# Gated cross attention and routed FFN on one core: small jobs put between the two halves of a step, numerators laid over denominators by DMA

## The chip, the cores and the metric

The kernel runs on one core of a Trainium2 chip, in one launch. The metric is the device time of the launch in microseconds (us). The core's engines are PE (TensorE, matrix products and transposes), ACT (ScalarE), DVE (VectorE), POOL (GpSimd) and SP (SyncE, which here only issues DMA transfers). Each engine carries out its own list of instructions in order; semaphores make one engine wait for another or for a DMA. Three times were taken of the kernel before: 714.03, 714.83 and 716.48 us, median 714.83.

## The reference, cut to what matters

`x` and `ctx` are 16 x 128 x 512 (batch, channel, position), float32.

```python
h = _layernorm(x)                     # over the 512 positions
qh = h.reshape(16, 8, 16, 512)        # 8 heads of 16 channels
kh = vh = ctx.reshape(16, 8, 16, 512)
sm = softmax(einsum('bhdq,bhdl->bhql', qh, kh) * scale, axis=-1)
ret = einsum('bhql,bhdl->bhdq', sm, vh).reshape(16, 128, 512)
x = x + tanh(g_xattn[0]) * gamma * ret
x = x + tanh(g_ffn[0]) * ffn(_layernorm(x))
```

`ffn` is a routed feed-forward block of eight experts, two per token, with a shared branch; the change doesn't touch it.

## The kernel before

**Stages.** The attention over 16 batches comes first and takes some 400 us; then the FFN for four groups of tokens. The change is in the attention.

**Windows.** Attention goes in windows w = 0 to 17 (with a short lead-in, w = -1). All engines run the same windows: `over_windows` lays out w = -1 to 3 one after the other, then a loop of five turns of two windows each (w = 4 to 13, the pair of bodies is that of w = 4 and 5), then w = 14 to 17. In window w a batch is at several stages at once: the maxima of batch w, the exponentials of batch w-1 (from step 7 of the window before on) and, one step behind them, its products with the values, the division and residual of batch w-2, the second layernorm of batch w-3, and keys and queries of batch w+1.

**A step on PE.** `pe_jobs` writes a window as eight steps s of two halves. A half step is: two matmuls of transposed scores (`st`), each into one of three PSUM slots called the ring; one pair of matmuls of scores in natural order (`nat`), of which DVE takes one row maximum `mx` (16 a window, k = 0 to 15, eight for each group g of heads); and four matmuls of exponentials with values (`pv`). In the step of the last keys of a group all eight `pv` come at the end of the step. Two other jobs use ring slots too: `m` transposes the 8 maxima of a group into a row, and `vt` transposes 128 x 512 context in two halves into values. ACT frees a ring slot: `st` by an exponential into `P`, `m` by writing `mrow` (times -1), which ACT then lays into row 48 of the query stack `QS` by DMA, `vt` by two copies into `VT` a half. PE waits for a slot that was used three jobs before (`ring_free`). The row of g = 0 is needed by the `st` of step 7 (ahead of k = 14), that of g = 1 by those of step 3 of the next window (k = 6). The order on ACT follows `pe_jobs`.

**Sums.** `VT` holds 16 columns of values and 16 of ones alternately, so that the sums `pv` hold in 32 partitions of a head pair 16 numerators and 16 equal denominators. For one group of heads the numerators are below, for the other above. ACT copies the sums of the two groups to `U0` and `U1`. SP stores the denominators (`den_scratch`), loads them back packed (`dc`), DVE takes the reciprocal after a fixed maximum (`PLACED`), SP stores it and loads it broadcast (`rd`). POOL masks both sums with `cme` (the gate in one half of the rows, 0 in the other) and adds them (`na`, `nb`, `num`), multiplies with `rd` (`att`), and adds `x` (`x1`).

**Order of the rest.** DVE puts its small jobs behind maxima by the table `PLACED`, POOL's list is `pool_jobs`, SP's is the body in `sync`. `Fori` loops run the two bodies with registers as indices. `tail` holds pieces of the second stage that are placed in the windows, on SP the zeroing of `y_sums` ("zeros"), four transfers a window from w = 3.

Of the kernel before, what the change touches and what calls it, by code (L numbers as in the profile page):

```python
# [28 lines left out]
P = 128  # L29
# [202 lines left out]
def attention(nc, c, keep, sb, ps, sem, x, ctx_kv, gx, gf, gamma, wall, const, ones, x1s, us, sq, sk, sd):  # L232
# [29 lines left out]
    cme = A("cme", [P, 2])  # L262
# [16 lines left out]
    t_st, t_xr, t_us = T("x1_out", 16), T("x_again", 16), T("u_out", 16)  # L279
    t_nat, t_ring, t_pv = T("pe_nat"), T("pe_ring"), T("pe_pv")  # L280
# [11 lines left out]
    def pe_jobs(w):  # L292
        jobs = []
        for s in range(STEPS):
# [11 lines left out]
            if s == 0 and 1 <= w <= B:  # L306
                jobs.append(("m", w - 1, 1))
            if s == 1 and w < B:
                jobs += [("vt", w, 0), ("vt", w, 1)]
            if s == 4 and w < B:  # L310
                jobs.append(("m", w, 0))
# [25 lines left out]
    def pool_jobs(w):  # L337
        jobs = []
        if 2 <= w < B + 2:
            jobs += [(w - 2, n) for n in ("na", "nb", "num")]  # L340
        if w + 1 < B:
            keys, queries = ("kh", "kl"), ("negm", "veps", "rstd", "rs", "qf", "qh", "ql")
            jobs += [(w + 1, n) for n in (("rstd",) if w < 0 else keys + queries)]
        if w >= 3:
            jobs += [(w - 3, n) for n in ("xnegm", "xveps", "xrstd", "u", "x1t")]
        if 0 <= w < B:
            jobs += [(w, "whi"), (w, "wlo")]
# [4 lines left out]
    for w in range(-1, B + 3):  # L352
# [15 lines left out]
        if 2 <= w < B + 2:  # L368
            t_ds.plan(w - 2, n=2)
            t_rb.plan(w - 2)  # L370
# [25 lines left out]
    def sync(sp, tail):  # L396
# [33 lines left out]
        def body(ck, w):  # L430
# [13 lines left out]
            if t >= 0:  # L444
                ck.wait(t_ev, t, 1)
                for g in range(2):
                    r = DH * (1 - g)
                    sp.dma_start(sd[ck.index(t), 0].rearrange("(j g) q -> g j q", g=2)[g], U[g][r:P:32, :]).then_inc(t_ds.sem, 16)
# [7 lines left out]
            if t >= 0:  # L456
                ck.wait(t_pool, t - 1, "x1")
                sp.dma_start(xr[:, :], x[ck.index(t)]).then_inc(t_xr.sem, 16)
# [28 lines left out]
            if 0 <= w and b < B:  # L487
                stack(ck, b, 0, 0)
            if s >= 0:
# [5 lines left out]
            if b < B:  # L495
                stack(ck, b, 1, 1)
                stack(ck, b, 1, 0)
# [96 lines left out]
    def scalar(act, tail):  # L594
# [20 lines left out]
        def value_sums(ck, b, s):  # L615
            ck.wait(t_pv, b, s)
            ck.wait(t_pool, b - 1, "nb")
            ck.wait(t_ds, b - 1)
            act.copy(U[s // 4][:, :], pv[:, :]).then_inc(t_ev.sem, 1)

        def body(ck, w):
# [3 lines left out]
            for kind, b, *rest in pe_jobs(w):  # L625
# [30 lines left out]
                else:  # L656
                    a, = rest
                    src = bank[:, 0:2 * P].rearrange("p (l j g d) -> p l g j d", l=2, g=2, d=DH)
                    for g in range(2):
                        m = act.copy(VT[i][:, 2 * a:2 * a + 2, g, :, DH * g:DH * g + DH], src[:, :, g, :, :])  # L660
# [9 lines left out]
    def vector(dve, tail):  # L670

        PLACED = {1: ("stats",), 2: ("aggr",), 5: ("recip",), 6: ("xstats",), 7: ("xaggr",)}
# [57 lines left out]
    def gpsimd(pool, tail):  # L730
        pool.memset(minus_half[:, :], -0.5).then_inc(t_vt.sem, 1)
        def job(ck, b, what):
# [3 lines left out]
            if what == "na":  # L736
                ck.wait(t_ev, b, 1)
                ck.wait(t_pool, b - 1, "att")
                done(pool.tensor_scalar(tn[:, :], U[0][:, :], cme[:, 0:1], 1.0, ALU.mult, ALU.mult))
            elif what == "nb":  # L740
                ck.wait(t_st, b - 2)
                done(pool.tensor_scalar(ao[i][:, :], U[1][:, :], cme[:, 1:2], 1.0, ALU.mult, ALU.mult))
            elif what == "num":
                ck.wait(t_pool, b, "nb")
                done(pool.tensor_tensor(tn[:, :], tn[:, :], ao[i][:, :], ALU.add))
            elif what == "att":
                ck.wait(t_rb, b)
                ck.wait(t_pool, b, "num")
                done(pool.tensor_tensor(ao[i][:, :], tn[:, :], rd[:, :], ALU.mult))  # L749
# [62 lines left out]
        def body(ck, w):  # L812
# [4 lines left out]
            if w < 0:  # L817
# [7 lines left out]
                pool.wait_ge(t_gate.sem, 2)  # L825

                pool.tensor_scalar(cme[:, 0:2], cst[:, K_ME:K_ME + 2], gate[:, 5:6], None, ALU.mult).then_inc(t_gate.sem, 1)
                pool.wait_ge(t_gate.sem, 3)
# [1436 lines left out]
```

## Time and profile before

| | us |
|---|---|
| median of three runs | 714.83 |
| lowest, highest | 714.03, 716.48 |
| profiled execution, its own time | 716.26 |
| its span in the trace | 714.4 |
| PE busy | 662.5 (93%) |
| ACT busy | 531.0 (74%) |
| DVE busy | 512.4 (72%) |
| POOL busy | 464.7 (65%) |

Busy times are for the whole span. In the attention windows all four engines are busy most of the time; in the second stage PE is, and the others less.

### The profile page before, as it was taken

What the parts mean: (1) busy time and instruction counts of PE and PEld (TensorE: products, weight loads), DVE (VectorE), ACT (ScalarE), POOL (GpSimd) and SP (SyncE); (2) the same over time, 40 slices, a digit from 0 to 9 for tenths busy, and PEclk for the clock granted to TensorE, in tenths of its full rate; (3) what the DMA queues carried; (4) which work ended last, traced back from release to release, by engine and by line L of the source; (5) the groups of instructions that cost most, each with busy time, mean ns of one, the idle gap of its engine ahead of it and who ended that gap; (6) DMA issues with size and microseconds to landing.
All of it is one profiled execution on the core that took longest, in us unless ns stands there. A gap on an engine that the chain in (4) does not pass through costs nothing. (4 is left out here: it accounts for less than half of the span.)

```text
span 714.4 us, 20683 instructions
## 1 busy us (share of the span) xinstructions
PE 662.5 (93%) x6005; PEld 352.7 (49%) x6005; DVE 512.4 (72%) x859; ACT 531.0 (74%) x1125; POOL 464.7 (65%) x464
## 2 busy tenths in 40 slices
PE   1798998899999999999999998879999999999998
PEld 0122222233333233322345554448999999998744
DVE  4988999899999999999878665564444444444456
ACT  2398998799999999999888467448777777677411
POOL 3557698888889888886846713404566665675622
PEclk9999999999999999999999999989999999999999
DMA  6646575656666566565334652448989779677587
GB/s 201 212 139 192 181 237 155 216 179 205 207 222 193 180 214 204 183 193 169 125 117 160 218 182 104 164 110 148 189 111 137 122 121 131 94 115 98 58 274 269
DMA packets 128176, 120.15 MB, mean 168 GB/s; under 512 B 64100, under 2 KB 97636, under 8 KB 128104
## 3 DMA queue, kind: packets, MB, share of 16 engines
q1 hardware_dynamic: 114680, 104.09, 50.1%
q0 software_dynamic: 12192, 14.16, 12.8%
q10 hardware_dynamic: 1232, 0.98, 0.4%
q8 instruction: 40, 0.66, 0.4%
q14 instruction: 32, 0.26, 0.1%
HBM read 60.25 MB, written 49.10 MB: 153 GB/s over the span
## 5 line engine op out<-in xcount | busy, mean ns | idle before, releaser
L716 DVE TENSOR_REDUCE mx<-nat 128x2 f32<-128x1024 f32 x256 | 296.6, 1213 | 24.3 <-PE nat L545 23.2
L641 ACT ACTIVATE P<-ring 128x512 f32<-128x512 f32 x512 | 279.4, 603 | 20.4 <-PE ring L557 10.4
L2229 POOL DMA_INDIRECT y_sums<-ysb,to x74 | 124.4, 1681 | 91.9 <-DVE ysb L2163 74.1
L570 PE MATMUL pv<-P,VT 128*32 128x256 f32 x2048 | 159.1, 395 | 0.4
L545 PE MATMUL nat<-KS,QS 48*128 48x512 f16 x512 | 111.9, 398 | 25.8 <-DMA QS<-q_scratch 15.0
L557 PE MATMUL ring<-QS,KS 49*128 49x512 f16 x512 | 123.5, 393 | 8.6 <-ACT P L641 8.6
L1331 PE MATMUL EH<-XA,whi 128*128 128x256 f16 (+1 forms) x688 | 104.5, 258 | 0.0
L1331 PE MATMUL Y<-whi,u 128*128 x592 | 104.0, 273 | 0.1
L570 PEld LDWEIGHTS pv<-P,VT 128*32 128x32 f32 x2048 | 44.1, 109 | 92.5 <-issue 44.6
L2113 DVE TENSOR_TENSOR u<-X,u 128x512 f16<-128x512 f32 x62 | 42.7, 689 | 64.6 <-ACT u L1737 64.6
L557 PEld LDWEIGHTS ring<-QS,KS 49*128 49x128 f16 x512 | 32.2, 93 | 111.7 <-ACT P L641 94.7
L1331 PE MATMUL EH<-XA,wlo 128*128 128x256 f16 (+1 forms) x344 | 84.5, 258 | 0.0
L1331 PE MATMUL Y<-wlo,u 128*128 x296 | 80.7, 273 | 0.0
L1731 ACT ACTIVATE X<-EH,bcur 128x256 f32<-128x256 f32 x124 | 63.2, 560 | 16.4 <-PE EH L1331 9.8
L1331 PEld LDWEIGHTS EH<-XA,whi 128*128 x688 | 64.0, 98 | 6.0
L1331 PEld LDWEIGHTS Y<-whi,u 128*128 128x128 f16 x592 | 57.9, 98 | 7.0 <-issue 0.3
L545 PEld LDWEIGHTS nat<-KS,QS 48*128 48x128 f16 x512 | 26.0, 95 | 39.1 <-DVE mx L716 21.9
L1737 ACT CAST u<-X 128x512 f16<-128x512 f32 x62 | 38.3, 618 | 5.1
L1331 PEld LDWEIGHTS EH<-XA,wlo 128*128 x344 | 33.6, 98 | 3.0
L1331 PEld LDWEIGHTS Y<-wlo,u 128*128 128x128 f16 x296 | 29.0, 98 | 3.2
L749 POOL TENSOR_TENSOR ao<-tn,rd 128x512 f32<-128x512 f32 x16 | 20.3, 1270 | 13.8 <-DMA rd<-den_scratch 13.6
L1745 ACT CAST uh<-Y 128x256 f16<-128x256 f32 x16 | 6.0, 372 | 30.8 <-PE Y L1580 30.8
(282 smaller groups left out, 1033.4 us busy)
## 6 DMA issues: line engine op xcount, KB each, us to landing
XA<-in_wall SPq DMA_DIRECT2D x8, 800.0 KB, 4.4
u<-in_wall SPq DMA_DIRECT2D x8, 800.0 KB, 4.4
QS<-q_scratch SPq DMA_DIRECT2D x64, 96.0 KB, 2.5
KS<-k_scratch SPq DMA_DIRECT2D x62, 96.0 KB, 2.2
X<-in_x SPq DMA_DIRECT2D x16, 256.0 KB, 2.8
q_scratch<-qhl SPq DMA_DIRECT2D x16, 256.0 KB, 2.1
xr<-in_x SPq DMA_DIRECT2D x16, 256.0 KB, 3.6
rd<-den_scratch SPq DMA_DIRECT2D x16, 256.0 KB
```

What stands on the lines that cost most here:

```text
L545: m = pe.matmul(nat[k % 2][:, a, :], QS[i][r, g, n, q0:q0 + P], KS[i][r, g, n, :], start=True, stop=True)
L557: pe.matmul(ring[place[key] % 3][:, :], KS[i][r, g, n, lb * P:lb * P + P], QS[i][r, g, n, :], start=True, stop=True).then_inc(t_ring.sem, 1)
L570: m = pe.matmul(pv[32 * j:32 * j + 32, q], VT[i][:, lb, g, j, :], Pb[4 * (s % 2) + j][:, q], start=(lb == 0 and half == 0), stop=(lb == 3) ...
L641: act.activation(Pb[4 * (s % 2) + j][:, :], bank[:, :], ACT.Exp).then_inc(t_use.sem, 1)
L716: dve.tensor_reduce(mx[:, k // 8, :, k % 8], nat[k % 2][:, :, :], AX.X, ALU.max).then_inc(t_max.sem, 1)
L749: done(pool.tensor_tensor(ao[i][:, :], tn[:, :], rd[:, :], ALU.mult))
L1331: m = pe.matmul(dst, l, r, start=first and n == 0, stop=last and n == 2, skip_group_check=skip)
L1731: m = act.activation(af[j % 2][:, tile, :], EH[j % 2][:, n, s * BLK:(s + 1) * BLK], ACT.Gelu, bias=bcur[:, j % 2, tile:tile + 1], scale=bc ...
L1737: act.copy(ah[j % 2][:, 2 * n:2 * n + 2, :], af[j % 2][:, 2 * n:2 * n + 2, :]).then_inc(t_ah.sem, 1)
L1745: act.copy(piece(oh, n), token(n)).then_inc(t_act.sem, 1)
L2113: dve.tensor_tensor(al[j % 2][:, 2 * n:2 * n + 2, :], af[j % 2][:, 2 * n:2 * n + 2, :], ah[j % 2][:, 2 * n:2 * n + 2, :], ALU.subtract).th ...
L2229: pool.indirect_dma_start(out=ysum[:, :], out_offset=bass.IndirectOffsetOnAxis(ap=to[:, j % 2, a:a + 1], axis=0), in_=ysb[j % 2][:, a, :], ...
```

## The change

On PE and ACT: the row of maxima of group 1 is transposed after the first half of step 1 instead of at the end of step 0; that of group 0 after the first half of step 5 instead of at the end of step 4; and the two halves of the values' transposes, which stood together at the end of step 1, follow one half step each. On ACT the copies into `VT` also multiply by the gate (`gate[:, 5:6]`, one value a partition), so the masks `cme` go. On DVE the small jobs of `PLACED` move. On POOL `na`, `nb` and `num` go; the splits of the weights (`whi`, `wlo`) come ahead of the second layernorm. The copy of the sums of group 0 goes to `U0` and `tn` in turn (`totals`), and four DMAs of 16 x 512 lay the numerators of group 1 over the denominators there. On SP these four are new, and the stacks of group 1 are loaded ahead of the stores of `u` and `x1`.

```diff
@@ attention
-    cme = A("cme", [P, 2])
+    t_nm = T("numerators_in", 16)
+    totals = lambda b, g: U[1] if g else (U[0], tn)[b % 2]
@@ pe_jobs, in the loop over the halves of step s
-            if s == 0 and 1 <= w <= B:
-                jobs.append(("m", w - 1, 1))
-            if s == 1 and w < B:
-                jobs += [("vt", w, 0), ("vt", w, 1)]
-            if s == 4 and w < B:
-                jobs.append(("m", w, 0))
+                if s == 1 and half == 0 and 1 <= w <= B:
+                    jobs.append(("m", w - 1, 1))
+                if s == 1 and w < B:
+                    jobs.append(("vt", w, half))
+                if s == 5 and half == 0 and w < B:
+                    jobs.append(("m", w, 0))
@@ pool_jobs
-        if 2 <= w < B + 2:
-            jobs += [(w - 2, n) for n in ("na", "nb", "num")]
...
+        if 0 <= w < B:
+            jobs += [(w, "whi"), (w, "wlo")]
         if w >= 3:
             jobs += [(w - 3, n) for n in ("xnegm", "xveps", "xrstd", "u", "x1t")]
-        if 0 <= w < B:
-            jobs += [(w, "whi"), (w, "wlo")]
@@ sync, body
-                    sp.dma_start(sd[...][g], U[g][r:P:32, :]).then_inc(t_ds.sem, 16)
+                    sp.dma_start(sd[...][g], totals(t, g)[r:P:32, :]).then_inc(t_ds.sem, 16)
...
                 ck.wait(t_pool, t - 1, "x1")
+                for r in range(DH, P, 32):
+                    sp.dma_start(totals(t, 0)[r:r + DH, :], totals(t, 1)[r:r + DH, :]).then_inc(t_nm.sem, 16)
                 sp.dma_start(xr[:, :], x[ck.index(t)]).then_inc(t_xr.sem, 16)
...
+            if b < B:
+                stack(ck, b, 1, 1)
+                stack(ck, b, 1, 0)
             if s >= 0:
                 ck.wait(t_pool, s, "u")
...
-            if b < B:
-                stack(ck, b, 1, 1)
-                stack(ck, b, 1, 0)
@@ scalar, value_sums
-            ck.wait(t_pool, b - 1, "nb")
-            ck.wait(t_ds, b - 1)
-            act.copy(U[s // 4][:, :], pv[:, :]).then_inc(t_ev.sem, 1)
+            if s // 4:
+                ck.wait(t_nm, b - 1)
+                ck.wait(t_ds, b - 1)
+            else:
+                ck.wait(t_pool, b - 2, "att")
+            act.copy(totals(b, s // 4)[:, :], pv[:, :]).then_inc(t_ev.sem, 1)
@@ scalar, body, values
-                        m = act.copy(VT[i][...], src[:, :, g, :, :])
+                        m = act.mul(VT[i][...], src[:, :, g, :, :], gate[:, 5:6])
@@ vector
-        PLACED = {1: ("stats",), 2: ("aggr",), 5: ("recip",), 6: ("xstats",), 7: ("xaggr",)}
+        PLACED = {0: ("stats",), 1: ("aggr",), 5: ("recip",), 8: ("xstats",), 9: ("xaggr",)}
@@ gpsimd, job
-            if what == "na": ...
-            elif what == "nb": ...
-            elif what == "num": ...
-            elif what == "att":
+            if what == "att":
                 ck.wait(t_rb, b)
-                ck.wait(t_pool, b, "num")
-                done(pool.tensor_tensor(ao[i][:, :], tn[:, :], rd[:, :], ALU.mult))
+                ck.wait(t_nm, b)
+                ck.wait(t_st, b - 2)
+                done(pool.tensor_tensor(ao[i][:, :], totals(b, 0)[:, :], rd[:, :], ALU.mult))
```

On PE, steps 0 and 1 of window 2, one of the windows that are laid out straight; before (`ring<-cst,mx` is the row of maxima, `ring<-cst,X` the values, `ring<-QS,KS` transposed scores):

```order
L570 MATMUL pv<-P,VT 32x256 x8
L580 MATMUL ring<-cst,mx 16x128
L557 MATMUL ring<-QS,KS 128x512 x2
L545 MATMUL nat<-KS,QS 128x512 x2
L570 MATMUL pv<-P,VT 32x256 x4
L557 MATMUL ring<-QS,KS 128x512 x2
L545 MATMUL nat<-KS,QS 128x512 x2
L570 MATMUL pv<-P,VT 32x256 x4
L589 MATMUL ring<-cst,X 128x128 x4
L557 MATMUL ring<-QS,KS 128x512 x2
L545 MATMUL nat<-KS,QS 128x512 x2
```

The same place in the changed kernel:

```order
L572 MATMUL pv<-P,VT 32x256 x8
L559 MATMUL ring<-QS,KS 128x512 x2
L547 MATMUL nat<-KS,QS 128x512 x2
L572 MATMUL pv<-P,VT 32x256 x4
L582 MATMUL ring<-cst,mx 16x128
L591 MATMUL ring<-cst,X 128x128 x2
L559 MATMUL ring<-QS,KS 128x512 x2
L547 MATMUL nat<-KS,QS 128x512 x2
L572 MATMUL pv<-P,VT 32x256 x4
L591 MATMUL ring<-cst,X 128x128 x2
L559 MATMUL ring<-QS,KS 128x512 x2
L547 MATMUL nat<-KS,QS 128x512 x2
```

The row of maxima moved behind the first pair of transposed scores of step 1, where it now stands beside the first half of the values; the second half stands a half step later.

On ACT, the same place; before:

```order
L641 ACTIVATE P<-ring 128x512 x3
L651 ACTIVATE mrow<-ring 16x128
L641 ACTIVATE P<-ring 128x512
L613 DMA QS<-mrow 2x8x128
L641 ACTIVATE P<-ring 128x512 x3
L660 COPY VT<-ring 128x2x4x16 x4
L641 ACTIVATE P<-ring 128x512 x9
```

and in the changed kernel:

```order
L646 ACTIVATE P<-ring 128x512 x5
L656 ACTIVATE mrow<-ring 16x128
L667 ACTIVATE VT<-ring,gate 128x2x4x16 x2
L646 ACTIVATE P<-ring 128x512
L615 DMA QS<-mrow 2x8x128
L646 ACTIVATE P<-ring 128x512
L667 ACTIVATE VT<-ring,gate 128x2x4x16 x2
L646 ACTIVATE P<-ring 128x512 x9
```

The row is written two exponentials later, and its DMA goes out behind the copies of the first half of the values; the copies are now an ACTIVATE with the gate as a second input.

On SP, with what each waits for, window 3, the end of its part that stores and loads; before:

```order
L486 DMA rd<-den_scratch 128x1x512 [waits pool,recip_out]
L404 DMA QS<-q_scratch 48x2x512 [waits pe_ring,q_out]
L404 DMA QS<-q_scratch 48x2x512
L491 DMA u_rows<-un 128x512 [waits pool]
L493 DMA x_rows<-ao 128x512 [waits pool]
L404 DMA KS<-k_scratch 48x2x512 [waits pe_ring,k_out]
L404 DMA KS<-k_scratch 48x2x512
L404 DMA QS<-q_scratch 48x2x512 [waits pe_ring,q_out]
L404 DMA QS<-q_scratch 48x2x512
L1209 DMA y_sums<-zs 128x2x256 [waits a_vt]
```

and in the changed kernel:

```order
L488 DMA rd<-den_scratch 128x1x512 [waits pool,recip_out]
L404 DMA QS<-q_scratch 48x2x512 [waits pe_ring,q_out]
L404 DMA QS<-q_scratch 48x2x512
L404 DMA KS<-k_scratch 48x2x512 [waits pe_ring,k_out]
L404 DMA KS<-k_scratch 48x2x512
L404 DMA QS<-q_scratch 48x2x512 [waits pe_ring,q_out]
L404 DMA QS<-q_scratch 48x2x512
L496 DMA u_rows<-un 128x512 [waits pool]
L498 DMA x_rows<-ao 128x512 [waits pool]
L1203 DMA y_sums<-zs 128x2x256 [waits a_vt]
```

The four loads of the stacks of group 1 stand ahead of the two stores. Further up in the same window, in the changed kernel:

```order
L428 DMA XA<-in_wall 128x1600 [waits pool]
L454 DMA dc<-den_scratch 128x32 [waits dve_small,den_out]
L459 DMA tn<-U 16x512 [waits pool]
L459 DMA tn<-U 16x512 x3
L460 DMA xr<-in_x 128x512
L424 DMA X<-in_ctx_kv 128x512 [waits pe_ring,pool]
```

The four numerators' DMAs stand between the load of `dc` and that of `xr`; before, nothing stood there.

## Rows read from the trace of the kernel before

**Rows 1.** One window, all engines: busy us (instructions), TensorE clock, DMA share, GB/s.
```profile
203.65:224.36 20.71, 19.95 (x203) 6.31 (x200) 19.85 (x22) 19.27 (x41) 18.37 (x22) 1.00 0.63 201
```

**Rows 2.** DVE timeline: start, us, engine, line, instruction [idle before <- ended by].
```profile
210.58 2.36 DVE L716 TENSOR_REDUCE mx<-nat 128x2 f32<-128x1024 f32 x2 [0.75 <-PE nat L545]
...
231.29 2.36 DVE L716 TENSOR_REDUCE mx<-nat 128x2 f32<-128x1024 f32 x2 [0.75 <-PE nat L545]
...
314.05 2.36 DVE L716 TENSOR_REDUCE mx<-nat 128x2 f32<-128x1024 f32 x2 [0.75 <-PE nat L545]
...
334.56 2.36 DVE L716 TENSOR_REDUCE mx<-nat 128x2 f32<-128x1024 f32 x2 [0.82 <-PE nat L545]
```

**Rows 3.** PE timeline, first half of the same window.
```profile
206.34 0.28 PE L580 MATMUL ring<-cst,mx 128*16 128x128 f32 x1
206.55 0.60 PE L557 MATMUL ring<-QS,KS 49*128 49x512 f16 x2
...
207.87 0.39 PE L557 MATMUL ring<-QS,KS 49*128 49x512 f16 x2
...
208.97 0.66 PE L589 MATMUL ring<-cst,X 128*128 128x128 f32 x4
209.56 0.76 PE L557 MATMUL ring<-QS,KS 49*128 49x512 f16 x2
...
211.04 0.39 PE L557 MATMUL ring<-QS,KS 49*128 49x512 f16 x2
```

**Rows 4.** ACT timeline, the same stretch.
```profile
205.11 1.60 ACT L641 ACTIVATE P<-ring 128x512 f32<-128x512 f32 x3
206.65 0.27 ACT L651 ACTIVATE mrow<-ring 16x128 f16<-16x128 f32 x1
207.05 0.60 ACT L641 ACTIVATE P<-ring 128x512 f32<-128x512 f32 x1
...
207.70 1.68 ACT L641 ACTIVATE P<-ring 128x512 f32<-128x512 f32 x3
209.45 0.77 ACT L660 COPY VT<-ring 128x128 f32<-128x128 f32 x4
```

**Rows 5.** ACT timeline, one line of the second stage (FFN).
```profile
542.59 1.51 ACT L1713 ACTIVATE X<-EH,bcur 128x128 f32<-128x128 f32 x4 [0.98 <-PE EH L1331]
```

**Rows 6.** PE timeline, middle of the window of rows 3.
```profile
215.56 0.39 PE L557 MATMUL ring<-QS,KS 49*128 49x512 f16 x1 [0.33 <-ACT P L641]
216.05 0.39 PE L545 MATMUL nat<-KS,QS 48*128 48x512 f16 x2
```

**Rows 7.** DVE timeline, the first two windows of the loop.
```profile
103.50 2.36 DVE L716 TENSOR_REDUCE mx<-nat 128x2 f32<-128x1024 f32 x2 [0.76 <-PE nat L545]
106.71 0.35 DVE L705 RECIPROCAL rc<-dc 128x32 f32<-128x32 f32 x1 [0.85 <-DMA dc<-den_scratch]
...
125.16 2.36 DVE L716 TENSOR_REDUCE mx<-nat 128x2 f32<-128x1024 f32 x2 [0.75 <-PE nat L545]
...
148.44 2.36 DVE L716 TENSOR_REDUCE mx<-nat 128x2 f32<-128x1024 f32 x2 [0.75 <-PE nat L545]
```

**Rows 8.** SP's queue, timeline, ahead of the loop.
```profile
96.52 2.02 SPq L1212 DMA_DIRECT2D y_sums<-zs  x4
...
99.71 1.33 SPq L448 DMA_DIRECT2D den_scratch<-U  x2
```

**Rows 9.** All engines in ten us of the second loop window.
```profile
130.00:140.00 10.00, 8.84 (x79) 2.58 (x83) 8.63 (x10) 6.95 (x15) 7.93 (x8) 0.83 0.51 162
```

**Rows 10.** Timeline of all engines after the last window.
```profile
401.58 0.25 DVE L2030 COPY acc<-Gp 128x16 f32<-128x16 f32 x2 [2.96 <-DMA x_rows<-ao]
...
403.14 0.39 PE L1331 MATMUL EH<-whi,guh 128*128 128x512 f16 x1 [0.61 <-DVE X L2035]
```

**Rows 11.** SP's queue in the window of rows 3: the weights' load.
```profile
207.12 0.34 SPq L428 DMA_DIRECT2D XA<-in_wall  x1
```

**Rows 12.** The page's list of DMA issues: KB each, us to landing.
```profile
XA<-in_wall SPq DMA_DIRECT2D x8, 800.0 KB, 4.4
```

More of the change, by code:

```diff
@@ L369, in attention @@
             t_ds.plan(w - 2, n=2)
+            t_nm.plan(w - 2, n=P // 32)
             t_rb.plan(w - 2)
@@ L447, in body @@
                     r = DH * (1 - g)
-                    sp.dma_start(sd[ck.index(t), 0].rearrange("(j g) q -> g j q", g=2)[g], U[g][r:P:32, :]).then_inc(t_ds.sem, 16)
+                    sp.dma_start(sd[ck.index(t), 0].rearrange("(j g) q -> g j q", g=2)[g], totals(t, g)[r:P:32, :]).then_inc(t_ds.sem, 16)
             if 2 <= w < B - 1:
@@ L657, in body @@
                     a, = rest
+                    if (w, a) == (0, 0):
+                        act.wait_ge(t_gate.sem, 2)
                     src = bank[:, 0:2 * P].rearrange("p (l j g d) -> p l g j d", l=2, g=2, d=DH)
                     for g in range(2):
-                        m = act.copy(VT[i][:, 2 * a:2 * a + 2, g, :, DH * g:DH * g + DH], src[:, :, g, :, :])
+                        m = act.mul(VT[i][:, 2 * a:2 * a + 2, g, :, DH * g:DH * g + DH], src[:, :, g, :, :], gate[:, 5:6])
                     m.then_inc(t_use.sem, 1)
@@ L735, in job @@
             v, m = ln[i], mv[i]
[L736 to L740, printed above, removed]
-                ck.wait(t_st, b - 2)
[L742 to L745, printed above, removed]
-            elif what == "att":
-                ck.wait(t_rb, b)
-                ck.wait(t_pool, b, "num")
-                done(pool.tensor_tensor(ao[i][:, :], tn[:, :], rd[:, :], ALU.mult))
+            if what == "att":
+                ck.wait(t_rb, b)
+                ck.wait(t_nm, b)
+                ck.wait(t_st, b - 2)
+                done(pool.tensor_tensor(ao[i][:, :], totals(b, 0)[:, :], rd[:, :], ALU.mult))
             elif what == "x1":
@@ L824, in body @@
                 pool.tensor_tensor(gate[:, 5:6], gate[:, 3:4], gate[:, 2:3], ALU.mult).then_inc(t_gate.sem, 1)
-                pool.wait_ge(t_gate.sem, 2)
-                pool.tensor_scalar(cme[:, 0:2], cst[:, K_ME:K_ME + 2], gate[:, 5:6], None, ALU.mult).then_inc(t_gate.sem, 1)
-                pool.wait_ge(t_gate.sem, 3)
         def last_norm():
@@ L876, in free_sums @@
     def free_sums(eng):
-        eng.wait_ge(t_pool.sem, t_pool.at[B - 1, "nb"])
+        eng.wait_ge(t_nm.sem, t_nm.value)
         eng.wait_ge(t_ds.sem, t_ds.value)
```

## The prediction

> **What bounds the kernel now.** I read the sums of one middle window first. In 20.71 us PE is busy 19.95, DVE 19.85, ACT 19.27 and POOL 18.37, at a granted clock of 1.00 [rows 1]: four engines within 8% of each other, so the sums can't say who paces. The waits can. DVE's timeline shows one wait of a window, 0.75 us at the fifth maximum, and it is ended by PE [rows 2]; the other maxima start as soon as PE has written them. So PE paces, and what PE's timeline shows as holes is what a window can lose. From one such wait to the next is the period: 210.58 to 231.29 is 20.71 in the loop, 314.05 to 334.56 is 20.51 behind it [rows 2]. A half step without a disturbance takes 1.10 on PE (207.87 to 208.97), the four transposes of the values 0.59 (208.97 to 209.56), and after them the next half step takes 1.48 instead of 1.10 (209.56 to 211.04) [rows 3], because a ring slot is still with ACT, which comes late to exponentials behind the row and four copies [rows 4]. That hole of 0.4 and the 0.21 at 206.34 are what the placement on PE can get at; 14 windows from w2 on have it.
>
> **The beginning of the window, with the new order.** All times are those of this window of before, moved.
> Pair c of scores starts at 206.34, 0.21 earlier than now [rows 3]. Its half step ends at 207.44; the row's transpose (0.21) and half of the values' (0.3) bring the next pair, d, to 207.96. ACT's first exponential comes 0.50 after the pair (206.55 to 207.05), the next 0.50 later ((1.60-0.60)/2), each 0.60 long [rows 3, 4]: the second of c ends at 207.94, and frees the slot of d's first just in time. The row (0.27 [rows 4]) frees that of d's second at about 208.15, so half step d starts 0.16 late and ends at 209.25. The copies of the first values end at 208.44 at their present pace; d's exponentials start at 208.45 and, with the row's DMA issue between (0.65, from 207.05 to 207.70 [rows 4]), at 209.10; the latter ends at 209.70, and its slot lets half step e start at 209.76 and end at 210.86. Before, it ended at 211.04 [rows 3]. **Gain 0.18 a window, if the copies cost what they cost now.**
>
> **The copies' price.** They won't. Four copies take 0.77 now [rows 4]; they become ACTIVATEs that read a factor from a column. No row shows that with these shapes. The nearest is the FFN's ACTIVATE of the same 128x128 size with a scale and a bias column: four take 1.51 [rows 5]. So one copy costs between nothing and (1.51-0.77)/4 = 0.185 more. I take the middle, 0.09, since the new one has one column and that row two. The first two copies lie on the chain above, so e moves by 0.19: 211.05, no gain. At 0.185 each, the window loses 0.19, and some 0.05 more from the second two.
> The Trainium skill ("ScalarE: Activation LUTs", section "What ACT_TABLE_LOAD costs") says that each one-column operand adds about 93 ns to an ACTIVATE; by it the sum would be the same as with my middle, no gain in the loop, though the edit saves nothing on ACT that was on the path. The row of the FFN, at twice that for two columns, agrees.
>
> **The middle.** PE waits 0.33 for an exponential (215.56), and the scores for the tenth maximum follow at 216.05, 0.49 later [rows 6], where they wait for DVE too, which has just done a small job. The second layernorm's small jobs go behind the ninth and tenth maximum, which takes DVE's part of that wait away; but the row of group 0 now comes between two pairs of scores, so that its slot wait moves there. Net 0; the bounds are the 0.33 gone, and 0.21 more for a transpose ahead of a pair that waits.
>
> **Loop and straight windows.** In the ten loop windows (w4 to w13) I take 0 (bounds -0.19 and +0.25). Behind and ahead of the loop (w2, w3, w14, w15) the same work takes 0.20 less [rows 2], so there is more slack under the dearer copies: an estimate of -0.15 each, -0.6 together (bounds -0.33 and 0 each).
>
> **POOL and DVE.** POOL loses `na`, `nb`, `num`, three instructions a window of its 22 [rows 1]. No wait in these rows is ended by POOL [rows 2, 3], so this is worth nothing. The new order puts the weights' splits earlier, and they wait for a load: issued at 207.12 [rows 11], landing 4.4 later [rows 12], 211.5, by when the queries' jobs ahead of them are still running. DVE's small jobs keep their durations. Nothing for either.
>
> **SP at the loop's entry.** SP's queue is in order. In w3 the stores of `u` and `x1` went out while the queue would have waited for PE's last use of the stacks anyway; now they stand behind the four loads that wait for it, so two issues come on top: of 0.34 [rows 11] to 0.50 (2.02 for four [rows 8]), 0.7 to 1.0 together. The four zeroing transfers and the denominators' store of w4 at 99.71 [rows 8] are behind them, and with that store `dc`. DVE already waits 0.85 for `dc` in w4 (106.71), and that window takes 21.66 (103.50 to 125.16) instead of 20.71: 0.95 lost for a wait of 0.85, so a late `dc` costs its lateness [rows 7]. The four new issues lie behind `dc` of the same window, but ahead of all that follows. I take +0.85 in w4 and, as an estimate, less than half of it, +0.35, in w5, where the queue has begun to catch up, together **+1.2** (bounds 0 and 2.5, the latter with another drop of the clock: w5 took 23.28 (125.16 to 148.44 [rows 7]) and its granted clock was 0.83 over ten us [rows 9], after the wait).
>
> **Tail.** After the last window DVE waits 2.96 for the last `x1` store and PE 0.61 behind it [rows 10]. That chain goes through the reciprocals' store and load of batch 15, past the four new issues on SP, 0.50 each [rows 8]; most pass while the reciprocals are still to come. I take **+0.4** (bounds 0 and 1.8, and -0.6 if the missing merge brings it forward).
>
> **Sum.** -0.6 + 0 + 1.2 + 0.4 = +1.0 on the profiled execution's 716.26 (span 714.4 and 1.9 around it), 717.3. That execution lies 1.43 above the median, so the median is forecast at **715.8**.
>
> **Rivals.**
> *The copies stay cheap* (faster). If the column is free, loop windows give 10 x 0.18 and the others 4 x (0.18 + 0.15), -3.1 in all: 714.83 - 3.1 = 711.7 with entry and tail unchanged; if in addition `dc` comes no later, or even sooner since POOL is ahead, the losses of w4 and w5 (0.95 + 2.57) go too, and it is 708. For it: copies are issued back to back, where a column might be fetched under the one before. Against it: 1.51 for four [rows 5] is just such a back to back row. With small losses at SP it takes in all that ends below 712.7: 0.22.
> *SP or the row of maxima is late* (slower). The step 3 scores need the row of group 1; that row is now written two exponentials later, and its DMA goes out behind two copies. That pair stood at 212.14 (211.04 and a half step [rows 3]) and, with the forecast's copies, stays there; the row, issued before with the exponential at 207.05 [rows 4], goes out at about 208.65. The queues carry the 800 KB of weights from 207.12 to 211.5 [rows 11, 12] just then. If the row lands more than 3.5 after its issue (it had 5.1), each window waits; with a wait of 0.5 in ten windows it is +5, or 720. The same price holds if SP's list, which gets four more issues a window (2.0 at 0.50 each [rows 8]), becomes longer than PE's period. Against it: no wait in rows 3 and 4 is ended by a DMA now. It decides from 0.2 us a window on (2.1 in ten). Chance 0.20.
> *Copies dearer* (slower). At 0.185 each, 10 x 0.25 + 0.4 outside, +2.9 on top: 718.7. Chance 0.12.
> *No effect* is my forecast's case: gains at the start of the window eaten by the copies, small losses at entry and tail. 0.46.
>
> **How the numbers follow.** What a measurement of this kernel can tell from no change is about 0.3%, 2.14 us: 712.69 to 716.97. Faster 0.22, within it 0.46, slower 0.20 + 0.12 = 0.32. The forecast's own terms reach from about 713.5 to 717.5. The range takes in the upper part of the rival with cheap copies (711.8) and the rival with dear ones (719.2), and leaves out the late row and the 708: about 0.1 each side.
>
> **What would show it.** On ACT, the copies `VT<-ring,gate`: together about 1.1 us for four (0.77 + 4 x 0.09), in two halves, would prove the middle price; 0.8 the cheap rival, 1.5 the dear one. On DVE, the period from one wait to the next: 20.7 in the loop. A wait of DVE for `dc` in w4 near 1.7 proves the entry's term; none there refutes it. A wait of PE for `QS<-mrow` ahead of the scores at step 3, or DMA named as what ends PE's waits every window, would prove the late row, and that would make the prediction wrong first; second, a clock below 1.00 in a window that shows 1.00 now, or a wait that the drop at w5 [rows 9] no longer has.

## The result

The changed kernel takes **723.61 us** in the median of six runs (720.68 to 728.13), the kernel before 714.79 (714.03 to 720.3); the ratio is 1.0129, with a 95% interval of 1.0087 to 1.017. So it is slower by 1.3%; 715.8 was forecast, in a range from 711.8 to 719.2. (A ratio here is the one on record with the runs; it differs a little from the quotient of the two medians, 1.0123.) Its profiled execution took 722.07, with a span of 720.2.

The page after, busy times and the groups that answer to those of before:

```profile
PE 662.9 (92%) x6005; PEld 353.3 (49%) x6005; DVE 515.2 (72%) x859; ACT 532.6 (74%) x1125; POOL 424.2 (59%) x415
...
L723 DVE TENSOR_REDUCE mx<-nat 128x2 f32<-128x1024 f32 x256 | 299.9, 1214 | 25.4 <-PE nat L547 24.1
L646 ACT ACTIVATE P<-ring 128x512 f32<-128x512 f32 x512 | 278.2, 600 | 34.8 <-PE ring L559 25.1
```

PE works as long as before (662.9 against 662.5 us). What was added is waiting. The view of waits, windows 4 to 15, says for what (engine, line, what ended the wait: us in total, times, longest):

```profile
DVE rc L712 <- DMA dc<-den_scratch: 5.8, 5, 3.3
...
PE nat L547 <- DMA QS<-q_scratch: 4.8, 5, 2.6
...
PE ring L559 <- DMA QS<-mrow: 3.0, 7, 0.8
```

Before, the same view of the same stretch has one row with a DMA on PE, ACT and DVE:

```profile
DVE rc L705 <- DMA dc<-den_scratch: 1.9, 2, 1.0
```

That was the loop's entry. Now three kinds of DMA are late: `dc`, the query stacks, and the row of maxima. DVE's timeline shows where; its rows at the loop's entry and two pairs of loop windows:

```profile
107.76 0.35 DVE L712 RECIPROCAL rc<-dc 128x32 f32<-128x32 f32 x1 [3.29 <-DMA dc<-den_scratch]
...
131.53 0.35 DVE L712 RECIPROCAL rc<-dc 128x32 f32<-128x32 f32 x1 [1.15 <-DMA dc<-den_scratch]
...
146.12 1.23 DVE L723 TENSOR_REDUCE mx<-nat 128x2 f32<-128x1024 f32 x1 [2.32 <-PE nat L547]
...
210.83 1.23 DVE L723 TENSOR_REDUCE mx<-nat 128x2 f32<-128x1024 f32 x1 [0.76 <-PE nat L547]
...
253.29 1.23 DVE L723 TENSOR_REDUCE mx<-nat 128x2 f32<-128x1024 f32 x1 [0.79 <-PE nat L547]
...
295.67 1.23 DVE L723 TENSOR_REDUCE mx<-nat 128x2 f32<-128x1024 f32 x1 [0.38 <-PE nat L547]
```

The reciprocal of w4 waits 3.29 instead of 0.85 [rows 7]. From 210.83 over 253.29 to 295.67, the first maximum of w9, w11 and w13, two windows take 42.46 and 42.38: 21.2 each instead of 20.71 [rows 2]. The windows, taken from the starts of their first maxima, in us, for the two profiled executions:

| | w0 to w3 | w4 | w5 | w6 to w13, mean | w14, w15 |
|---|---|---|---|---|---|
| before | 83.4 | 21.57 | 23.28 | 20.71 | 20.60, 20.57 |
| changed | 82.1 | 25.94 | 24.14 | 21.25 | 20.68, 20.42 |

The sum is +8.1 at the end of the maxima (349.07 and 357.18): +5.2 in w4 and w5, +4.3 in the eight windows after them, -1.3 ahead of the loop and -0.1 behind it. The -1.3 is no gain to count on: in a second pair of traces, below, it is +0.4. The spans differ by 5.8 only; the rest comes back in the second stage, which the change doesn't touch. PE of the changed kernel is 9.3 us behind at its first products after the wait for the last `x1` store, 7.2 some twelve us later and 5.6 from 490 on. The last 1.5 of this belong to a place where PE's granted clock was 0.66 over ten us in the kernel before; the changed kernel has a smaller such place:

```profile
470.00:480.00 10.00, 5.85 (x29) 4.00 (x29) 7.31 (x24) 2.18 (x4) 0.00 (x0) 0.66 0.44 107
```

```profile
100.00:110.00 10.00, 7.09 (x68) 2.25 (x66) 6.07 (x7) 7.62 (x17) 7.94 (x7) 0.98 0.59 181
110.00:120.00 10.00, 9.62 (x79) 2.38 (x79) 8.28 (x10) 6.21 (x12) 3.05 (x5) 0.68 0.49 159
480.00:490.00 10.00, 8.62 (x64) 7.08 (x65) 5.47 (x9) 3.48 (x9) 0.00 (x0) 0.83 0.60 150
```

The first two of these rows are the loop's entry after: behind the wait for `dc`, with PE busy 7.09 of 10 us, the clock is at 0.68 in the next ten, so PE ran mostly at the lower of its levels (1.2 GHz) just when it had to catch up. Before, this stretch had 1.00, and the drop came a window later and smaller (0.83 [rows 9]).

SP's queue, one loop window of the changed kernel (start, us, line, DMA, count); the gaps between rows are either small issues left out or waiting:

```profile
275.83 1.38 SPq L448 DMA_DIRECT2D den_scratch<-U  x2
...
279.16 2.49 SPq L459 DMA_DIRECT2D U<-U  x4
...
283.85 0.35 SPq L479 DMA_DIRECT2D k_scratch<-khl  x1
286.75 0.89 SPq L404 DMA_DIRECT2D KS<-k_scratch  x2
...
297.01 0.65 SPq L448 DMA_DIRECT2D den_scratch<-tn  x1
```

From one store of denominators to the next it is 21.18 (275.83 to 297.01). The four numerators' issues take 2.49, that is 0.62 each. Behind the stores of the keys (the last issued at 283.85, the issue done at 284.20) the queue stands until 286.75, for those stores to land. In the kernel before:

```profile
205.45 1.34 SPq L448 DMA_DIRECT2D den_scratch<-U  x2
...
208.74 0.33 SPq L458 DMA_DIRECT2D xr<-in_x  x1
209.77 0.33 SPq L424 DMA_DIRECT2D X<-in_ctx_kv  x1
211.71 0.35 SPq L476 DMA_DIRECT2D k_scratch<-khl  x1
212.26 0.35 SPq L477 DMA_DIRECT2D k_scratch<-khl  x1
214.42 0.89 SPq L404 DMA_DIRECT2D KS<-k_scratch  x2
...
226.16 1.33 SPq L448 DMA_DIRECT2D den_scratch<-U  x2
```

There the queue stood 0.7 at 209.07 and 1.6 at 210.10, ahead of the keys that POOL was still making, and its landing took 1.8 (212.61 to 214.42); the period was PE's, 20.71. Summed over all rows of one such window, SP's issues take 10.1 us before and 12.6 after, and the gaps between them 10.6 and 8.6. The largest gap left, 2.55, is a landing of its own, and those ahead of the context's load and the keys' stores are 0.37 and 0.31: SP waits for no other engine's work there. SP's view of waits says the same of all windows from w6 to w13: in the changed kernel every wait is for a landing of its own, 23.7 us in all, and in the kernel before 19.2 us were for POOL, ACT and PE besides, the largest for the keys:

```profile
SPq L116 <- POOL khl L803: 9.1, 7, 1.3
```

The list has become the slowest thing in the loop. What it delivers late is waited for. On PE:

```profile
282.19 0.54 PE L559 MATMUL ring<-QS,KS 49*128 49x512 f16 x2 [0.78 <-DMA QS<-mrow]
...
295.24 0.39 PE L547 MATMUL nat<-KS,QS 48*128 48x512 f16 x2 [0.33 <-DMA QS<-q_scratch]
```

The first is the row of maxima ahead of k = 6 of w12; the second the query stack of w13's first scores.

### The profile page after: what moved, and what is told of

Read it like the earlier page. It is cut to its first block, busy times and chain, and to the rows that moved or that the text cites. A ratio compares the mean times of both kernels' runs of the same rounds, so it can differ in the third digit from the quotient of the medians.

```text
span 720.2 us, 20651 instructions
## 1 busy us (share of the span) xinstructions
PE 662.9 (92%) x6005; PEld 353.3 (49%) x6005; DVE 515.2 (72%) x859; ACT 532.6 (74%) x1125; POOL 424.2 (59%) x415
## 4 chain that ended last, share of the span: by engine, by line
PE 47%; DMA 17%; SPq 9%; DVE 8%; issue 7%; POOL 7%; ACT 3%; another core or an unknown queue 1%; POOLq 0%; DVEq 0%; ACTq 0%
PE EH L1325 21%; PE Y L1325 15%; PE pv L572 4%; DMA k_scratch<-khl 4%; DMA rd<-den_scratch 4%; DVE mx L723 4%; PE ring L559 3%; SPq L404 2%; SPq L459 2%; DMA q_scratch<-qhl 2%; DMA QS<-q_scratch 2%; PE nat L547 1%; ACT P L646 1%; DMA den_scratch<-U 1%; POOL ao L747 1%
## 5 line engine op out<-in xcount | busy, mean ns | idle before, releaser
L723 DVE TENSOR_REDUCE mx<-nat 128x2 f32<-128x1024 f32 x256 | 299.9, 1214 | 25.4 <-PE nat L547 24.1
L547 PE MATMUL nat<-KS,QS 48*128 48x512 f16 x512 | 115.0, 399 | 30.4 <-DMA QS<-q_scratch 19.8
L559 PE MATMUL ring<-QS,KS 49*128 49x512 f16 x512 | 122.5, 394 | 10.4 <-ACT P L646 6.5
L559 PEld LDWEIGHTS ring<-QS,KS 49*128 49x128 f16 x512 | 34.1, 93 | 111.9 <-ACT P L646 92.7
L547 PEld LDWEIGHTS nat<-KS,QS 48*128 48x128 f16 x512 | 26.1, 95 | 42.8 <-DVE mx L723 20.7
L747 POOL TENSOR_TENSOR ao<-U,rd 128x512 f32<-128x512 f32 x8 | 10.2, 1269 | 31.2 <-DMA rd<-den_scratch 31.2
```

What stands on the lines that cost most here:

```text
L547: m = pe.matmul(nat[k % 2][:, a, :], QS[i][r, g, n, q0:q0 + P], KS[i][r, g, n, :], start=True, stop=True)
L559: pe.matmul(ring[place[key] % 3][:, :], KS[i][r, g, n, lb * P:lb * P + P], QS[i][r, g, n, :], start=True, stop=True).then_inc(t_ring.sem, 1)
L723: dve.tensor_reduce(mx[:, k // 8, :, k % 8], nat[k % 2][:, :, :], AX.X, ALU.max).then_inc(t_max.sem, 1)
L747: done(pool.tensor_tensor(ao[i][:, :], totals(b, 0)[:, :], rd[:, :], ALU.mult))
```

## The experiments

Each ratio below is to executions of the kernel before on the same chip at the same time. The kernels were measured in four groups, each on a chip of its own. The kernel before took 703 us on three of these chips and 715 on that of `zeros_late`, `rows_back`, `no_num_rows_zeros` and `before_zeros_late`, as in the first measurement. Most of that difference is in the second stage, since its attention ends at 346.0 and 349.1 in the two traces. So only ratios are compared, and windows of attention. The ratios differ by up to 0.24% from the quotients of the medians (1.0113 against 1.0089 for `zeros_late`), so differences of that size between two groups say nothing.

The expectations name their explanations by letters. A: the four new issues make SP's list longer than PE's period. B: the row of maxima is late, because its DMA was moved. C: the dearer copies. D, from `zeros_late` on: the loss is at the loop's entry, where `dc` is late.

**Four more issues alone** (`extra_issues`), in the kernel before:

```diff
                 ck.wait(t_pool, t - 1, "x1")
+                ck.wait(t_nm, t - 1)
+                for r in range(DH, P, 32):
+                    sp.dma_start(spare[r:r + DH, :], U[1][r:r + DH, 0:P]).then_inc(t_nm.sem, 16)
```

> The kernel before with four more DMAs a window on SP at the place of the numerators (16 rows of 128 columns of U1 into a spare tile that nobody reads), nothing else changed. Theory A: SP's list becomes the longest in the loop, period above 20.9, dc comes later in each window, total 719 to 724. Theory B or C: no difference, 714 to 716, since SP has slack.

1.0283 (1.0243 to 1.0324), 722.0 against 702.8. Loop windows 21.83 in the mean, w4 24.83, w5 22.68. SP's timeline:

```profile
214.01 2.49 SPq L463 DMA_DIRECT2D spare<-U  x4
...
218.62 0.35 SPq L483 DMA_DIRECT2D k_scratch<-khl  x1
222.22 0.89 SPq L407 DMA_DIRECT2D KS<-k_scratch  x2
```

The issues cost the same 2.49 with a quarter of the bytes, and the keys' landing is waited for 3.25 us. Theory A is right that SP had no room for four. The total overstates it: ACT's copy of the sums had to wait for these DMAs too, and at the end it stood 4.91 us for one, w15 taking 26.96:

```profile
354.35 0.58 ACT L626 COPY U<-pv 128x512 f32<-128x512 f32 x1 [4.91 <-DMA spare<-U]
```

**The placement alone** (`placement`): the edits of `pe_jobs` and of `PLACED` as in the change, in the kernel before.

```diff
-            if s == 0 and 1 <= w <= B:
-                jobs.append(("m", w - 1, 1))
...
+                if s == 1 and half == 0 and 1 <= w <= B:
+                    jobs.append(("m", w - 1, 1))
...
-        PLACED = {1: ("stats",), 2: ("aggr",), 5: ("recip",), 6: ("xstats",), 7: ("xaggr",)}
+        PLACED = {0: ("stats",), 1: ("aggr",), 5: ("recip",), 8: ("xstats",), 9: ("xaggr",)}
```

> The kernel before with only the jobs on PE (and so on ACT) and on DVE placed as in the change. Theory A: no wait for a DMA in the loop, 712 to 715, since the copies have their old pace and each loop window may win up to 0.18. Theory B: waits for QS<-mrow as in the changed kernel, 717 or more.

1.0064 (1.0044 to 1.0084): slower, against theory A as I had put it. Loop windows 21.35. The waits are mostly for `QS<-q_scratch` and `dc`, little for the row. The trace says where they begin. From w6 to w13 POOL waits 7.0 us for DVE's statistics of the second layernorm, which now come two maxima later (2.3 before), and SP waits twice as long for POOL's keys as before:

```profile
SPq L116 <- POOL khl L803: 18.5, 8, 3.5
```

That the later statistics are the cause was not tried by itself.

**Without the numerators' DMAs** (`no_numerators`): that, and the change's new order on POOL and SP.

```diff
+            if b < B:
+                stack(ck, b, 1, 1)
+                stack(ck, b, 1, 0)
             if s >= 0:
                 ck.wait(t_pool, s, "u")
```

> The changed kernel's placement on PE, ACT and DVE and its new order on POOL and SP, but with the merge on POOL (na, nb, num), plain copies into VT and no numerators' DMAs. Theory A (the four new issues make SP's list longer than PE's period): loop windows back to 20.7 or less, at most the entry's loss left, total 713 to 716. Theory B (the row of maxima is late because its DMA was moved): PE still waits for QS<-mrow in loop windows, total 719 or more. Theory C (the copies with the gate): about 720, less only what the copies cost.

1.0050 (1.0028 to 1.0073), loop windows 21.01. A large part of the loss is gone, but not all; in the loop five waits for `QS<-mrow` are left (2.4 us from w6 to w13), against one for the stacks (0.3). So theory B holds for what is left in the loop, some 1.8 us over eight windows. The entry is as bad without the new DMAs: w4 and w5 take 25.24 and 20.65, 3.0 more than in `before_again`.

**The issues on POOL** (`pool_issues`), in the changed kernel:

```diff
-                for r in range(DH, P, 32):
-                    sp.dma_start(totals(t, 0)[r:r + DH, :], totals(t, 1)[r:r + DH, :]).then_inc(t_nm.sem, 16)
...
+                if w >= 2 and k[1] == ("whi" if w < B else "xnegm"):
+                    ck.wait(t_ds, w - 2)
+                    ck.wait(t_ev, w - 2, 1)
+                    ck.wait(t_pool, w - 3, "x1")
+                    for r in range(DH, P, 32):
+                        pool.dma_start(totals(w - 2, 0)[r:r + DH, :], totals(w - 2, 1)[r:r + DH, :]).then_inc(t_nm.sem, 16)
```

> The changed kernel with the four numerators' DMAs issued by POOL ahead of the weights' split instead of by SP. Theory A: SP's list is as long as before, loop period about 20.5 to 20.7, total 713 to 717 (a little above if POOL's issues are slow). Theory B: the row stays late, 719 or more. Theory C: 719 or more.

1.0101 (1.0055 to 1.0147), loop windows 21.07. The waits from w6 to w13:

```profile
PE ring L557 <- DMA QS<-mrow: 2.3, 5, 0.8
...
DVE rc L710 <- DMA dc<-den_scratch: 0.5, 1, 0.5
```

No wait for a stack is left there; the rows remain. Four issues on POOL take 2.09, less than the merge that they replaced (0.69 + 0.69 + 1.28 us in the kernel before):

```profile
253.26 2.09 POOL L815 DMA_DIRECT2D tn<-U  x4
255.34 1.53 POOL L802 CAST whi<-u 128x1600 f32 x1
```

**The two kernels again, on one chip** (`before_again`, `changed_again`).

> The kernel before, unchanged, for its trace beside the runs of this chip. If the chip of the last four runs is used, about 703; the difference to 715 then lies in the FFN (PE busy 43 of 50 us from 450 on in the first trace), and the loop windows show 20.7 without a wait for a DMA.

> The changed kernel, unchanged, beside the kernels of this chip. Theory A+B (SP's list is as long as the window, and the rows of maxima are late besides): 1.2 to 1.6% above the kernel before, as first measured, loop windows 21.2 in the mean, waits for QS<-q_scratch, dc and QS<-mrow.

701.73, and for the changed kernel 714.09 and 1.0162 (1.0145 to 1.0179). Their traces differ by 13.1 at the end of the maxima (345.96 and 359.05): w4 27.13 against 21.98 and w5 24.38 against 20.88, 8.6 together; w6 to w13 171.5 against 166.3, 5.2; w14 and w15 40.2 against 41.2. The entry is where most goes in this pair. The windows view of w4 of the changed kernel:

```profile
105.00:110.00 5.00, 2.37 (x21) 0.76 (x24) 3.48 (x4) 3.53 (x7) 3.66 (x2) 0.85 0.60 186
110.00:115.00 5.00, 5.00 (x37) 1.14 (x33) 3.33 (x6) 1.88 (x4) 2.11 (x5) 0.50 0.34 109
```

PE works 2.37 of five us, and has half its clock for the next five.

**Rows back, numerators on POOL** (`pool_rows_back`), and **rows back, without numerators** (`no_num_rows_back`). Both have this, on `pool_issues` and on `no_numerators`:

```diff
-                if s == 1 and half == 0 and 1 <= w <= B:
-                    jobs.append(("m", w - 1, 1))
                 if s == 1 and w < B:
                     jobs.append(("vt", w, half))
-                if s == 5 and half == 0 and w < B:
-                    jobs.append(("m", w, 0))
+            if s == 0 and 1 <= w <= B:
+                jobs.append(("m", w - 1, 1))
+            if s == 4 and w < B:
+                jobs.append(("m", w, 0))
```

> The changed kernel with the numerators' DMAs issued by POOL and the two rows of maxima transposed where the kernel before does it (ends of steps 0 and 4). Theory B (rows late because moved): no wait for QS<-mrow is left in the loop, and it gains about 2 us on the variant with POOL's issues alone (ratio 1.010), so 1.003 to 1.008. Theory A alone: the rows' waits came from a busy queue, and the ratio stays at 1.010.

> The variant without numerators' DMAs (merge on POOL, plain copies, new placement and new SP and POOL order) with the two rows of maxima back at the ends of steps 0 and 4. Theory B: no wait for QS<-mrow, loop windows 20.5 to 20.8, ratio 0.995 to 1.000 (that variant had 1.005). Otherwise 1.005 again.

1.0011 (0.9991 to 1.0031) and 0.9982 (0.9963 to 1.0). Loop windows 20.60 and 20.58, no wait for a row from w6 to w13. Both pairs differ by the rows alone: 1.0101 to 1.0011 and 1.0050 to 0.9982, 0.9 and 0.7%. Theory B holds in both. But w4 is 24.24 and 27.16 even here.

**Rows back, numerators still on SP** (`rows_back`): the same edit in the changed kernel.

> The changed kernel with only the two rows of maxima back at the ends of steps 0 and 4, numerators still issued by SP. Theory B (rows): no wait for QS<-mrow, ratio 0.6 to 0.9 of a per cent lower than 1.016, as in the two pairs of variants without SP's issues. If SP's list alone paces (theory A), the same ratio with longer waits for QS<-q_scratch.

1.0195 (1.0148 to 1.0242), not lower than the changed kernel's 1.0129 and 1.0162. From w6 to w13:

```profile
PE nat L547 <- DMA QS<-q_scratch: 10.4, 6, 3.2
...
DVE rc L712 <- DMA dc<-den_scratch: 1.4, 2, 0.8
```

The rows' waits are gone, and those for the stacks have grown from 4.6 to 10.4 in the same view of the changed kernel on its second chip. With SP's list as the slowest, a row that comes earlier gives nothing: theory A as expected for this case. Part of the 1.0195 is something else: w6 took 25.11 in the trace, with a granted clock of 0.50 from 145 to 155. But w8 to w13 are no shorter either, 21.72 in the mean against 21.41 in `changed_again`.

**Zeroing late** (`zeros_late` on the changed kernel, `no_num_rows_zeros` on `no_num_rows_back`, `before_zeros_late` on the kernel before):

```diff
             if w == 3:
                 sp.wait_ge(t_vt.sem, 4)
-                tail["spare zeros"]()
-                for n in range(3):
-                    tail["zeros"](ck, n)
             if 3 <= w < B:
                 tail["zeros"](ck, w)
+            if w == B - 1:
+                tail["spare zeros"]()
+                for n in range(3):
+                    tail["zeros"](ck, n)
```

> The changed kernel with the five extra zeroing DMAs at the end of window 3 on SP moved to the end of window 15. Theory D (the loop's entry costs most: dc late in w4, DVE and PE stand, PE's clock drops to half): the wait for dc in w4 falls from 2.5 us to below 1, w4 from 27 to about 21 to 22, and the ratio from 1.016 to 1.005 to 1.009. Theory A alone (SP's list is too long in every window): only the 3.5 us of issues shift, the queue is late again one window on, ratio 1.012 to 1.016.

> The variant without numerators' DMAs and with the rows back (0.998) and the five zeroing DMAs late. Theory D: its w4 of 27.2 us falls to about 21, ratio 0.988 to 0.993, faster than the kernel before. Otherwise 0.998.

> The kernel before with only the five zeroing DMAs late. Theory D: dc isn't late in w4 and w5, which are 22.0 and 20.9 on this chip, so 0.5 to 1.5 us less, ratio 0.997 to 1.000.

1.0113 (1.0073 to 1.0154), **0.9923** (0.9892 to 0.9953) and 0.9966 (0.9936 to 0.9996). (One of the ten executions of `before_zeros_late` took 2128.44 us; it isn't in the ratio.) w4 is 21.36, 20.47 and 20.62: the wait for `dc` in w4 is gone in all three. w5 is mended only in part in the first two: 22.77 and 22.37, with `dc` late there by 1.56 and 0.68 (21.29 and 0.11 in the third). In the changed kernel the loss then comes in the windows behind, whose mean from w6 to w13 is 21.45:

```profile
247.99 0.39 PE L548 MATMUL nat<-KS,QS 48*128 48x512 f16 x2 [1.84 <-DMA QS<-q_scratch]
...
290.99 0.39 PE L548 MATMUL nat<-KS,QS 48*128 48x512 f16 x2 [1.13 <-DMA QS<-q_scratch]
```

So each theory was half right: with the zeroing `dc` is late in w4, and the list is too long in every window. `no_num_rows_zeros` beats both kernels: 709.66 against 715.47.

**Half of the numerators** (`two_issues`), in `zeros_late`; the numerators of the other half are left out:

```diff
-                for r in range(DH, P, 32):
+                for r in range(DH, P, 64):
```

> The variant with late zeroing DMAs (the changed kernel otherwise, ratio 1.011) with only two of the four numerators' DMAs issued by SP; the other half of the numerators is left out of the computation. If SP's list paces the loop, its 1.2 us fewer issues give most of that back in each of the windows w5 to w13: loop windows from 21.6 to 20.7 to 21.0, ratio 0.999 to 1.004. If what paces is the landing of the numerators or the rows of maxima, it stays at 1.008 or more.

1.0022 (0.9997 to 1.0047) against 1.0113 with four, on another chip. From w6 to w13 the only waits of PE, ACT or DVE for a DMA are these:

```profile
PE ring L560 <- DMA QS<-mrow: 3.8, 5, 1.1
```

SP itself waits for other engines again in these windows, which it never does there in `zeros_late`, with four:

```profile
SPq L116 <- PE ring L560: 6.2, 8, 1.4
SPq L116 <- ACT U L625: 3.0, 4, 1.2
```

So with two issues its list has room. But the loop got hardly shorter, and there the expectation failed: w6 to w13 are 21.28 in the mean, not 20.7 to 21.0, and with w5 (23.50, `dc` late by 1.47 and a granted clock of 0.86 and 0.80 over five us each behind it) the nine windows have 21.53 against 21.59 with four. The rows (3.8 us) have come up in place of the stacks, as in `pool_issues`. The fall of the ratio is more than the two traces show.

**All three mended, the change's idea kept** (`pool_rows_zeros`): numerators on POOL, rows back, zeroing late; and the same **with plain copies** (`plain_copies`), which leaves the gate out of the computation:

```diff
-                        m = act.mul(VT[i][...], src[:, :, g, :, :], gate[:, 5:6])
+                        m = act.copy(VT[i][...], src[:, :, g, :, :])
```

> The change's idea kept (numerators laid by DMA, gate in the copies), with the three losses taken out: numerators issued by POOL, rows of maxima at the old place, zeroing DMAs late. Loop windows 20.6 or less, w4 below 22, ratio 0.993 to 0.999.

> The last kernel with plain copies into VT instead of ACTIVATEs with the gate; the gate is left out of the computation. At 362 against 279 ns a copy, four a window: if the copies are on the path as the prediction has it, 0.1 to 0.2 us a window, 1.5 to 3 us in all (0.2 to 0.4%) less than that kernel; if not, the same.

**0.9939** (0.9912 to 0.9965) and 0.9908 (0.9871 to 0.9944). The first has windows of 20.60 from w6 to w13 and w4 at 20.47, and this is the only row of waits of PE, ACT or DVE for a DMA there (its profiled execution, 704.2, is the slowest of six whose median is 700.6):

```profile
DVE rc L711 <- DMA dc<-den_scratch: 0.3, 1, 0.3
```

The copies, in the list of groups (busy us, mean ns):

```profile
L666 ACT ACTIVATE VT<-ring,gate 128x128 f32<-128x128 f32 x64 | 20.1, 365 | 8.8 <-issue 4.7 <-PE ring L590 3.5
```

```profile
L666 ACT COPY VT<-ring 128x128 f32<-128x128 f32 x64 | 13.9, 269 | 9.5 <-issue 4.8 <-PE ring L590 4.2
```

365 against 269 ns a copy, and the windows 20.60 against 20.50: 0.1 a window. The intervals of the two ratios overlap, so the total alone doesn't show the price; the dear copies of theory C are the smallest of the losses.

**The old order of SP's stores** (`old_sp_order`), in the changed kernel: the stores of `u` and `x1` ahead of the loads again.

> The changed kernel with the stores of u and x1 ahead of the loads of the stacks of group 1 again. If the moved stores are what makes dc late at the loop's entry: w4 from 26 to 27 down by about 0.9, and the ratio by 0.1 to 0.3% from 1.013 to 1.016. If u comes late from POOL in its new order, the queue stands behind that store and it gets slower instead.

1.0171 (1.0117 to 1.0226), the same as 1.0162 within its interval; w4 26.48 and w5 21.53 against 27.13 and 24.38, but the mean from w6 to w13 is 21.69 against 21.44. DVE's wait for `dc` in w4 is 3.55, as long as ever. The moved stores don't make the loss.

## Why the prediction was wrong

**Two terms of the sum failed: the loop at 0, where the four new issues had no price, and the entry at +1.2.** In the first pair of traces they measured +4.3 (w6 to w13) and +5.2 (w4 and w5), in the second +5.2 and +8.6.

**The loop.** "Loop and straight windows" took 0 there, and the issues entered the sum only at the entry ("behind `dc` of the same window") and in the tail. The length of SP's list stood in the rival *SP or the row of maxima is late*, with a chance of 0.20 and the argument against it that no wait in the rows was ended by a DMA. That argument was weak. It said that SP wasn't late, and not how much room it had: I had read one issue and one load of its queue [rows 8, 11], and not a window. One window read whole gives the room: of the 10.6 us of gaps 8.6 stay when the queue never waits for others, so 2.0 were room, and four issues take 2.49. They were also priced at 0.50 each from the zeroing [rows 8], and take 0.62. `extra_issues` and `two_issues` show it from both sides: with four issues more SP waits for nobody but its own transfers, with two (1.25) it waits for PE and ACT again. The room alone isn't the whole loss: without any of the four on SP (`pool_issues`, `no_numerators`) the windows are still 21.07 and 21.01, and fall to 20.60 and 20.58 only with the rows back.

**Both halves of that rival were true, and not side by side.** The row of group 1 was to be late if it landed more than 3.5 us after its issue: at w12 it was issued at 277.73 and PE went on at 282.19, 4.5 later:

```profile
277.17 0.27 ACT L656 ACTIVATE mrow<-ring 16x128 f16<-16x128 f32 x1
277.34 0.59 ACT L667 ACTIVATE VT<-ring,gate 128x128 f32<-128x128 f32 x2
277.73 0.52 ACTq L615 DMA_DIRECT2D QS<-mrow  x1
...
279.06 0.63 ACT L667 ACTIVATE VT<-ring,gate 128x128 f32<-128x128 f32 x2
```

Where SP has the numerators, putting the rows back gives nothing (`rows_back`); where it has not, it gives 0.7 to 0.9%.

**Entry: right place, wrong size.** `dc` late in w4 was the term, +1.2 for w4 and w5; it is +5.2 in the first pair and +8.6 in the second. A wait of DVE near 1.7 was named as the proof; it is 3.29. The load of `dc` in w4 is issued 5.2 us after the first maximum of w4 (97.36) in the kernel before and 7.1 after it (96.04) in the changed one:

```profile
102.52 0.34 SPq L454 DMA_DIRECT2D dc<-den_scratch  x1
```

```profile
103.12 0.33 SPq L454 DMA_DIRECT2D dc<-den_scratch  x1
```

In the second pair it is 5.5 and 7.1. So the issue is 1.6 to 1.9 later against its window, where 0.7 to 1.0 was forecast. The moved stores, my cause, are not it: with the old order the load is at 7.1 too. Nor are the numerators, with 7.0 in `no_numerators`. The five zeroing transfers that stand ahead of it in both kernels are needed for it: with them late it is 3.5 (`zeros_late`). Which of the change's edits turns them into a loss wasn't found; the placement alone has 6.3 and a w4 of 23.05. The sum also took the lateness once, and the clock came on top: ten us at 0.68 are 3.2 us at the full clock, an estimate.

**The copies: right.** "Together about 1.1 us for four" are 0.59 to 0.63 for two, so 1.2 for four; 362 ns is the mean against 279. The middle price held, and it costs 0.1 a window where it could be read, not 0.19. The Trainium skill's figure ("ScalarE: Activation LUTs", section "What ACT_TABLE_LOAD costs", about 93 ns for each one-column operand) agrees with 365 less 269, 96 ns.

**The beginning of the window: not shown.** The gain of 0.18 was to come from the row of group 1 moved behind the first pair. In the loop that move made the row late, and with it back where it was the loop got faster in both pairs of kernels. With the rows back, no numerators and late zeroing the mean from w6 to w13 is 20.50, with the merge on POOL and plain copies, against 20.72 of `before_zeros_late`. These 0.22 a window come from the split values, the places on DVE and the new order together, and not from the forecast's mechanism; the three weren't taken apart.

**Tail: about as forecast.** PE of the changed kernel is 8.4 us behind at the end of its last products with values and 9.3 behind after the wait for the last `x1` store in the first pair, where DVE's wait for it is 4.61 instead of 2.96; in the second pair it is 13.4 and 13.8, with 2.98 in both. That is +0.9 and +0.4; +0.4 was forecast.

**What stays open.** Why loop windows of even number take about 1.5 us more than odd ones in the changed kernel (22.01 and 20.42 for w12 and w13) was not tried; which edit makes `dc` late in w4 is open, as said; and how much of the clock's drop in w4 is the wait's doing is only argued from their order in time.

## What to carry to other kernels

Before an issue goes onto a queue, read one whole period of that queue and add up the time in which it waits for another engine's work; that is its room, and the absence of waits for DMAs elsewhere doesn't show it. A transfer that replaces work of an engine may go onto that engine's queue: with the rows back, the same four DMAs stood at 1.0195 on SP and at 1.0011 on POOL, and with late zeroing POOL's kernel (0.9939) is within the intervals of the one without them (0.9923). And where a window is laid out anew, look first at the largest single wait: here DVE waited 2.4 us longer for `dc` (3.29 against 0.85), a drop of the clock followed, and the two windows lost 5.2.

## What was not expected of the hardware

The four small SBUF to SBUF transfers take SP 0.62 us each with 2 KB a row and with 512 bytes a row alike (2.49 for four in both), though the same queue issues others in 0.34. On POOL the four take 2.09. A wait for `dc` of 3.29 us was followed by a granted clock of 0.68 over ten us, one of 2.51 by 0.50 over five; these windows (w4) took 4.4 and 5.2 us more than before.
